# Conditioned residual on one core: a quarter of one pair in eight is loaded by GpSimd in a shape of 8 by 4, beside a tiny load

## What is computed

```python
x = x + einsum('bct,bcd->bdt', x, L0_cond_weights[itok_B_1_198])
x = x + einsum('bct,bcd->bdt', x, L1_cond_weights[itok_B_0_7]) + fside_8xS_0[itok_B_0_7][:, :, None]
```

## Time and profile before

| | us |
|---|---|
| median of 3 runs | 352.03 (350.30 to 352.62) |
| profiled execution | 353.64 |
| span of the profile | 351.9 |
| DMA traffic in it | 140.80 MB, mean 400 GB/s |

### The profile page before, as it was taken

One profiled execution on the slowest core, in us unless ns is written; L12 is line 12 of the kernel. 1 busy time (PEld: TensorE's weight loads), 2 busy tenths in 40 slices (PEclk: granted clock), 3 DMA queues, 4 the chain that ended last, 5 costly groups with the idle time before them and its releaser, 6 DMA issues.

```text
span 351.9 us, 5351 instructions
## 1 busy us (share of the span) xinstructions
PE 281.1 (80%) x774; PEld 135.6 (39%) x774; DVE 126.3 (36%) x202; ACT 97.0 (28%) x135; POOL 65.3 (19%) x249
## 2 busy tenths in 40 slices
PE   2898499859959977985985996998399678686894
PEld 2454245324424533532532533443155233342341
DVE  3354134404423522441541541444035334342441
ACT  1133035302413321520341331443034212232232
POOL 2400041113113112212212212330131121221200
PEclk9999789969978988998998996999789999999998
DMA  7999999999999999999999999999999999999966
GB/s 282 372 414 422 410 401 413 405 407 403 427 423 424 417 399 419 408 420 386 377 424 415 422 425 422 424 424 420 424 390 401 425 422 415 424 377 415 401 261 247
DMA packets 32554, 140.80 MB, mean 400 GB/s; under 512 B 3617, under 2 KB 15266, under 8 KB 16418
## 3 DMA queue, kind: packets, MB, share of 16 engines
q1 hardware_dynamic: 23184, 74.14, 53.7%
q10 hardware_dynamic: 9362, 66.59, 45.2%
HBM read 76.03 MB, written 67.11 MB: 407 GB/s over the span
## 4 chain that ended last, share of the span: by engine, by line
SPq 44%; DMA 36%; issue 9%; PE 8%; ACT 1%; ACTq 0%
DMA xy<-x 27%; SPq L113 16%; SPq L131 13%; DMA out<-xy 8%; SPq L108 8%; PE y_ps L254 8%; SPq L114 4%; SPq L128 3%; PE m_ps L237 1%; ACT xy L350 1%; DMA cond_words<-cond 0%; SPq L149 0%; ACTq L359 0%; SPq L124 0%; ACTq L358 0%
## 5 line engine op out<-in xcount | busy, mean ns | idle before, releaser
L254 PE MATMUL y_ps<-xy,m_sb 128*128 128x512 f32 x512 | 257.2, 640 | 53.1 <-DMA xy<-x 52.0
L254 PEld LDWEIGHTS y_ps<-xy,m_sb 128*128 128x128 f32 x512 | 96.6, 204 | 162.4 <-issue 130.9
L350 ACT ACTIVATE xy<-y_ps,j_pick 128x512 f32<-128x512 f32 x128 | 88.0, 687 | 236.7 <-PE y_ps L254 236.5
L326 DVE TENSOR_SCALAR xy<-y_ps,j_pick 128x512 f32<-128x512 f32 x128 | 96.1, 751 | 156.3 <-PE y_ps L254 156.3
L188 POOL COPY w_pick<-w_home 128x128 f32 x112 | 32.9, 293 | 258.2 <-issue 258.2
L237 PEld LDWEIGHTS m_ps<-j_pick,w_pick 128*128 128x128 f32 x224 | 37.3, 209 | 30.9 <-issue 30.5
L318 DVE TENSOR_TENSOR m_sb<-m_ps,j_pick 128x256 f32<-128x256 f32 x64 | 27.2, 424 | 57.4 <-PE m_ps L237 54.5
L237 PE MATMUL m_ps<-j_pick,w_pick 128*128 128x128 f32 x224 | 37.0, 291 | 0.0
L190 POOL COPY j_pick<-j_all 128x129 f32 x112 | 33.0, 295 | 0.1
L237 PE MATMUL m_ps<-j_pick,w_home 128*128 128x128 f32 x32 | 6.5, 338 | 10.0 <-issue 6.0
L350 ACT ACT_TABLE_LOAD x7 | 9.0, 1283 | 13.7 <-POOL j_pick L202 7.4
(11 more groups left out here) (16 smaller groups left out, 2.8 us busy)
## 6 DMA issues: line engine op xcount, KB each, us to landing
xy<-x SPq DMA_DIRECT2D x63, 1024.0 KB, 22.0
out<-xy ACTq DMA_DIRECT2D x63, 1024.0 KB, 9.2
w_home<-w_t SPq DMA_DIRECT2D x128, 64.0 KB
xy<-x SPq DMA_DIRECT2D x4, 256.0 KB, 22.8
j_all<-w_bias SPq DMA_DIRECT2D x1, 516.0 KB, 3.4
out<-xy SPq DMA_DIRECT2D x2, 256.0 KB, 4.4
out<-xy ACTq DMA_DIRECT2D x2, 256.0 KB, 4.1
cond_words<-cond ACTq DMA_DIRECT2D x1, 1.0 KB
```

The lines of the kernel that those rows point to most:

```text
L254: nc.tensor.matmul(y_ps[:, b % YB, h, :], m_sb[:, s, k, :], xy[:, s, k, half(h)], start=True, stop=True).then_inc(y_ready, 1)
L326: nc.vector.tensor_scalar(xy[:, s, k, half(0)], y_ps[:, b % YB, 0, :], j_pick[:, s, k, D:D + 1], None, ALU.add).then_inc(left_out[b % YB], 1)
L350: nc.scalar.activation(xy[:, s, k, half(1)], y_ps[:, b % YB, 1, :], ACT.Identity, bias=j_pick[:, s, k, D:D + 1]).then_inc(right_out[b % YB ...
```

## The change

In rounds 1 to 7 the pair of buffer `SHARED` = 3 is loaded in two parts. SyncE loads partitions 0 to 95 (`load_most`, `MOST` = 96), counted on `x_loaded[3]` as before. GpSimd, after its pick of that pair, issues a load of 8 rows of 64 B into a buffer `spill` that nothing reads, and then the load of partitions 96 to 127, whose source is viewed as 8 by 4 rows; it is counted on a semaphore of its own. Two of the 8-row loads are issued once ahead of the loop. TensorE waits for the new semaphore before it uses the pair, and GpSimd waits, ahead of each of the 8-row loads, for all that went before. Round 0 and the other seven buffers are as they were.

```diff
+    SHARED = 3
+    MOST = C - C // 4
...
+        spill = sb("spill", [8, 2, 16])
...
+        rest_loaded = sem("rest_loaded")
+        spilled = sem("spilled")
...
+            def load_most(r, s):
+                sp.dma_start(xy[0:MOST, s, :, :].rearrange("c k t -> c (k t)"),
+                             x_v[bass.ds(r * RING + s, 1), 0:MOST, :].rearrange("n c f -> (n c) f"))\
+                  .then_inc(x_loaded[s], 16)
...
                     sp.wait_ge(stored[s], r * 16)
-                    load_x(r, s)
+                    (load_most if s == SHARED else load_x)(r, s)
...
                 sp.wait_ge(stored[s], (ROUNDS - 1) * 16)
-                load_x(ROUNDS - 1, s)
+                (load_most if s == SHARED else load_x)(ROUNDS - 1, s)
...
+            def load_rest(r, s):
+                nc.gpsimd.dma_start(spill[:, 0, :], x[0, 0:8, 0, 0:16]).then_inc(spilled, 16)
+                nc.gpsimd.dma_start(
+                    xy[MOST:C, s, :, :].rearrange("c k t -> c (k t)"),
+                    x_v[bass.ds(r * RING + s, 1), MOST:C, :].rearrange("n (e c) f -> (n e) c f", e=8))\
+                  .then_inc(rest_loaded, 16)
...
             pool.wait_ge(home_ready, 4)
+            for i in range(2):
+                nc.gpsimd.dma_start(spill[:, i, :], x[0, 0:8, 0, 0:16]).then_inc(spilled, 16)
             with pool.Fori(1, ROUNDS) as r:
                 for s in range(RING):
 
                     pool.wait_ge(stored[s], r * 16)
+                    if s == SHARED:
+                        pool.wait_ge(spilled, r * 16 + 16)
                     pick(r, s)
+                    if s == SHARED:
+                        load_rest(r, s)
...
                 if k == 0:
+                    if s == SHARED and not first:
+                        pe.wait_ge(rest_loaded, r * 16)
                     if not last:
                         pe.wait_ge(x_loaded[s], r * 16 + 16)
```

## The result

The changed kernel takes 369.31 us (median of 4 executions, 365.61 to 371.79) against 352.32 (350.30 to 353.06) for the kernel before on the same chip. The ratio is 1.0481, with a 95% interval of 1.0412 to 1.0551: 17 us slower, which is 2.4 us for each of the seven rounds that the change touches. The profiled execution of after took 368.57 us, with a span of 366.9.

What follows compares the result with a forecast made beforehand. The prediction took the sixteen DMA engines as the bound, with one late engine setting the end. Rows saved, -4.3 us, plus small packets, +0.7, gave -3.6: 352.0 became 348.4 us, with a range of 346.8 to 357.0.

Steps and rivals of the forecast that it cites:

- the side that had been given 0.27: Whole kernel: chance of being more than 1% slower, made up of rival (a) at 0.22 and rival (c) at 0.05.
- The bound: Whole kernel: the sixteen DMA engines limit it, with a DMA share of 1.01 to 1.02 at 403 to 422 GB/s.
- Failed step one: GpSimd's 32-row load, rounds 1 to 7: always the same eight engines serve it, the late engine not among them; -4.3 us.
- -4.3 us: Late engine, seven rounds: two rows fewer a round, 14 rows in all at 0.309 us each.
- rival (a): Rounds 1 to 7: the 32 rows fall on the eight holding the late engine, +4.3 and 0.7 us, 357.0; chance 0.22.
- Failed step two: SyncE's 96-row load, rounds 1 to 7: 6 rows an engine at 0.309 us each, nothing added for loads beside it.
- Rival (b): Cut loads: rows dealt over sixteen, or meetings at write places eat the gain; middle 352, worst +2.9 us; chance 0.17.
- the late engine: Kernel's tail: one DMA engine of sixteen still works at full rate while fifteen have nothing; its last rows set the end.
- GpSimd's issue: GpSimd, two DMA issues a round at 0.43 us each: 0.9 us a round, 0 on the path; 6 us without cover.
- rival (c): PE's wait for the shared pair: GpSimd's part lands last, up to +8 less 3.6 us, 356; chance 0.05.
- The small packets: Late engine, seven rounds: one tiny-load row and two completion messages a round at 0.032 us each, +0.7 us; bounds 0 and 6.5.
- theory W: From the experiments: which partitions counts; p and p + 32 within a half of 64 share a write place, the halves don't.

Runs made afterwards that it cites:

- The two experiments that change the order of the halves: One 8-row load ahead of the loop instead of two: against the changed kernel, 370.34 us; in the cut by columns with GpSimd, 350.85 us.

## Why the prediction was wrong

The forecast was 348.4 us with a range of 346.8 to 357.0. The time was 369.31, outside the range, on the side that had been given 0.27.

**The bound** was read rightly: it is the DMA engines, and nearly all of the loss came through them. But the prediction measured what they can do by their busy share. A share near 1 was true of before (422 GB/s) and is true of the dents of after (234 to 246 GB/s). So an engine that waits in the middle of a row counts as busy: between 98 and 104 us a row of SyncE's takes 0.55 us on average, ahead of it 0.31. The share tells whether an engine has work, and the bytes beside it tell whether it gets on.

**Failed step one: "I take eight engines, always the same eight".** The 32 rows in 8 by 4 ran on all sixteen, from GpSimd (share 1.05) and from SyncE (1.04). The two experiments that change the order of the halves moved nothing. With this step -4.3 us was gone, and rival (a) as well.
**Failed step two, which made the 17 us: the price of SyncE's 96 rows, 6 x 0.309 us an engine, with nothing for the loads beside them.** The row price of 0.309 comes from loads over all 128 partitions, and the prediction carried it over to a load that covers others. A 96-partition load alone runs at 240 GB/s where one of 128 has 417, so its rows cost 1.7 times as much. In the changed kernel its rows took 0.34 to 0.64 us on average, by round, and rows of the whole loads next to it were held up with them: 7.0 and 6.6 us over the seven rounds. GpSimd's 32 rows, alone at 197 GB/s or 2.1 times the price, kept the plain price in the kernel, 0.31 us in five of seven rounds.

What the loads alone say of a cut pair can be held against what the kernels lost (from the ratios, divided by the rounds or pairs). Prices: 128 rows 1.05 MB / 417 GB/s = 2.5 us; 96 rows 0.79 / 240 = 3.3; 32 rows 1.3; 0 to 63 0.52 / 231 = 2.3; 64 to 127 2.5 (whole); 32 to 95 0.52 / 364 = 1.4.

| the pair is loaded as | sum less 2.5 | measured, us a pair |
|---|---|---|
| 96 + 32, both SyncE | 3.3 + 1.3 - 2.5 = 2.1 | 1.7 |
| 96 + 32, GpSimd's 8 by 4 (after) | 2.1 | 2.4 |
| 64 + 64 | 2.3 + 2.5 - 2.5 = 2.3 | 2.2 |
| 32 to 95, 0 to 31, 96 to 127 | 1.4 + 1.3 + 1.3 - 2.5 = 1.5 | 1.4 |
| four times 32 | 4 x 1.3 - 2.5 = 2.7 | 2.1 |
| by columns | 0 | 0.0, -0.1 |

The sums are made of loads that ran alone and are rough: the same 64 rows, 0 to 63, had 231 GB/s inside in one run and 184 in another, and with 184 the third sum would be 2.9. The second line fits for the wrong reason, too. GpSimd's rows, priced at 1.3 here, took the plain price in the kernel, about 0.6 us for two rows an engine, while the 128-row loads beside the cut one, priced at nothing, lost nearly as much as it did. What the table does show is that the cuts by columns cost nothing and every cut by partitions something, least where one part is 32 to 95.

**Rival (b) named the mechanism** ("where two write to one place at the same time each row takes longer") **and had its size wrong.** It priced the meetings only for the 42 rows of the late engine, at half a row price at worst: 6.5 us. The trace of after has the 96 rows held up by 0.1 to 1.1 of a row price, 0.54 on average, which is 7.0 us and close to that worst case; what the rival left out is the 6.6 us of the 128-row loads beside them. It also took them off a gain of 3.6 us that never came. The argument against it, that q1 "leaves half of each write path free", is one about the mean over a load with all partitions, and says nothing of a load that leaves some of the paths out altogether. By the Trainium skill (SBUF — State Buffer, section "Door 1: The DMA port swizzle") a load's rate depends on how many of sixteen ports its partitions reach. With 184 GB/s inside for partitions 0 to 63 and 369 for 32 to 95 the traces agree. They show too that the number of ports is not all: 0 to 95 and 0 to 111 lie on both sides of the middle as 0 to 127 does, and alone they take 3.86 and 4.08 us where 128 rows take 3.49. The section was cited as support for a rival with a chance of 0.17 where it could have led to a price for each part of the cut.

**What was right or harmless.** Bytes and queues: 7 x 256 KB on a third queue, as predicted. GpSimd's issue: 0.52 us for the tiny load and 0.51 for the other against 0.43 taken, and hidden, as GpSimd's own idle time stayed at 258.6 us. The line of GpSimd's load and what waited for it:

```profile
L206 POOL DMA_DIRECT2D xy<-x x7: 505/505/519, 53.8 to 324.4; - x7
...
  PEld y_ps L279: 4.1, 1
...
DMA to landing us min/median/max: 5.4/8.2/9.8
```

It lands in 8.2 us against 26.9 for SyncE's part. Once in seven rounds a weight load waited 4.1 us for it, so rival (c) exists but decided nothing: the column cut has the same wait in TensorE's code and loses nothing. The small packets (0.7 us) can't be told from the scatter.

**The late engine.** Its part in the tail of before stands as the rows show it, but it was the wrong place to look, since 14 of 15 us were lost ahead of the last loads.

**Open.** Why one engine is late at the end of the kernel before: a load of 128 rows alone has none that lags (share 0.98), and no shape was found that takes rows off it. Why the loads of 96 and 112 rows are longer alone than 128: by theory W the half of the places that holds 0 to 63 gets as many rows as with 128, which would make them as long, not longer. Why the cut load is held up in some rounds and hardly in others, and why the loads beside it suffer. GpSimd's 32 rows beside whole loads cost 0.8 us a round where 1.3 was their price alone; in that trace they took 0.31 to 0.32 us each in six of seven rounds, so there they hardly met, and no run was made to show why. And no version was found that beats the kernel before: the three column cuts are equal to it (ratios 0.9985 to 1.0004).

## What to carry to other kernels

When a load into SBUF is split over queues or in time, split it by columns, so that each part still covers all 128 partitions: the same bytes and queues cost nothing by columns (ratio 1.0004) and 4.8% by partitions. Read the rate beside the DMA share, since a share of 1 at 240 GB/s is a bound of another kind than a share of 1 at 420. A price taken from one shape of load is a price for that shape; where a change alters which partitions a load reaches, the price has to be measured or bounded from the slowest load in sight, and not taken from the mean.

## What the runs showed that was not expected

- Fewer partitions can take longer in plain time: alone, 128 rows 3.49 us, 112 rows 4.08, 96 rows 3.86.
- In the changed kernel the cut load holds up its neighbours too: 6.6 us of held-up rows in whole loads of 128 beside 7.0 in the loads of 96, against 1.9 and 0.6 in the same places before.
- Partitions 32 to 95 take data at twice the pace of 0 to 63 in the middle of the load (369 and 358 against 184 GB/s), though the whole loads take the same 2.3 us. Over the whole load partitions 0 to 31 have 183 GB/s and 0 to 63 have 195, so 32 to 63 add rows but hardly any pace to 0 to 31. What adds pace is the other side of the middle.
- A source viewed as 8 by 4 neighbouring rows was served by all sixteen engines (share 1.05 and 1.04).
- GpSimd's DMAs were issued in 0.51 to 0.52 us each and the 256 KB loads landed, beside the others, 5.4 to 9.8 us later, while SyncE's 1 MB took 23.6 behind their backlog.
